# The order of four engines in a memory-attention stage, and who makes two of eight final clips

## The reference, cut to what matters

```python
xi = layernorm(hidden) @ Wq.T                       # 8 heads
for _ in range(3):                                  # NUM_STEPS
    scores = einsum('bhsd,hnd->bhsn', xi, K) * beta # 256 memory slots per head
    w = entmax15(scores)                            # = square(clip(x - tau, 0))
    xi = einsum('bhsn,hnd->bhsd', w, V)
out = xi.transpose(0, 2, 1, 3).reshape(B, S, H * hd) @ Wo.T
# entmax15: tau is the threshold at which sum(square(clip(x - tau, 0))) == 1
```

## Time and profile before

| | us |
|---|---|
| median of three runs | 1848.6 |
| the three runs | 1848.60, 1849.27, 1843.72 |
| profiled execution, its own time | 1844.72 |
| profiled execution, span | 1842.9 |
| first `centre` (unit 0) to last `centre` (unit 47) within the span | 512.02 to 1288.80 |

### The profile page before, as it was taken

The page is one execution under the profiler, slowest core; times in us unless marked ns, Lnnn a source line. Parts: engine busy times, 40 slices in busy tenths (PEclk is TensorE's granted clock), DMA queues, the critical chain, the costliest instruction groups (busy, mean ns, idle before and its releaser), DMA issues. The chain is left out here.

```text
span 1842.9 us, 25960 instructions
## 1 busy us (share of the span) xinstructions
PE 1595.7 (87%) x7554; PEld 1120.9 (61%) x7554; DVE 1375.4 (75%) x3613; ACT 1181.6 (64%) x2865; POOL 601.2 (33%) x1908
## 2 busy tenths in 40 slices
PE   5799999989748889978898879888879899999987
PEld 2546656565646667866786668766645556555554
DVE  6666757562359999999999999999744565776646
ACT  3244343412159999999999999999637665665630
POOL 3504233240134455545554455544310100101000
PEclk9799999999888889999998889988989999999989
DMA  5000000000300000000000000000000000000000
GB/s 227 1 1 1 1 1 1 1 1 0 109 1 1 1 1 1 1 1 1 1 1 1 1 1 1 1 1 1 1 0 1 1 1 1 1 13 1 12 1 23
DMA packets 6717, 19.23 MB, mean 10 GB/s; under 512 B 1072, under 2 KB 4144, under 8 KB 5296
## 3 DMA queue, kind: packets, MB, share of 16 engines
q1 hardware_dynamic: 6576, 17.58, 2.6%
HBM read 15.48 MB, written 2.10 MB: 10 GB/s over the span
## 5 line engine op out<-in xcount | busy, mean ns | idle before, releaser
L1610 ACT ACTIVATE mem_arena<-mem_arena,r_shift 128x256 f32<-128x256 f32 x864 | 385.2, 511 | 23.0 <-POOL r_shift L1529 23.0
L1340 DVE BATCH_NORM_STATS2 r_moments<-mem_arena 128x6 f32<-128x512 f32 x576 | 379.9, 690 | 9.4 <-ACT mem_arena L1610 6.3
L1689 PE MATMUL r_bank<-arena,r_wT 128*128 128x256 f32 x1024 | 232.3, 386 | 4.2 <-ACT mem_arena L1610 3.7
L1689 PEld LDWEIGHTS r_bank<-arena,r_wT 128*128 128x128 f32 x1024 | 195.1, 194 | 35.3 <-issue 9.0
L1705 PE MATMUL r_bank<-ident,mem_arena 128*128 128x128 f32 x576 | 109.6, 322 | 71.8 <-DVE mem_arena L1356 71.7
L1317 DVE MAX8 r_top<-r_bank 128x8 f32<-128x256 f32 x384 | 145.3, 405 | 17.1 <-PE r_bank L1689 16.9
L1699 PE MATMUL r_bank<-arena,ident 128*128 128x256 f32 x384 | 142.4, 458 | 12.6 <-ACT r_wT L1636 12.4
L2243 ACT ACTIVATE arena<-arena,e_NM 128x512 f32<-128x512 f32 (+3 forms) x256 | 134.3, 558 | 29.5 <-DVE e_NM L1931 29.5
L1705 PEld LDWEIGHTS r_bank<-ident,mem_arena 128*128 128x128 f32 x576 | 79.8, 164 | 114.1 <-DVE mem_arena L1356 104.6
L1689 PE MATMUL r_bank<-arena,r_xnT 128*128 128x256 f32 x512 | 120.8, 396 | 24.1 <-ACT mem_arena L1610 23.7
L1610 ACT ACTIVATE r_u<-r_u,r_shift 128x256 f32<-128x256 f32 x288 | 131.8, 510 | 5.6 <-POOL r_shift L1529 5.6
(11 more groups left out here) (328 smaller groups left out, 3222.1 us busy)
## 6 DMA issues: line engine op xcount, KB each, us to landing
w<-in_w SPq DMA_DIRECT2D x3, 1024.0 KB, 14.4
out_x<-X SPq DMA_DIRECT2D x4, 512.0 KB, 2.9
X<-in_x SPq DMA_DIRECT2D x1, 1536.0 KB, 10.6
w_in<-in_w_in SPq DMA_DIRECT2D x1, 1156.0 KB, 6.4
mem_arena<-in_wq SPq DMA_DIRECT2D x1, 1024.0 KB, 17.5
mem_arena<-in_wo SPq DMA_DIRECT2D x1, 1024.0 KB, 21.0
gate<-in_gate SPq DMA_DIRECT2D x1, 1024.0 KB, 7.8
up<-in_up SPq DMA_DIRECT2D x1, 1024.0 KB, 9.8
```

Of the source, the lines that this page charges most:

```text
L1340: last = dve.bn_stats(moments[:, a.lane, 2 * p:2 * p + 2, :].rearrange("p two c -> p (two c)"), u[a.lane][:, 2 * p:2 * p + 2, :].rearrange ...
L1610: last = act.activation(u[a.lane][:, h, :], u[a.lane][:, h, :] if k else scores[:, h, :], ACT.Relu, bias=shift[:, a.lane, h:h + 1])
L1689: last = pe.matmul(scores[:, h, :], lhs, (G1 if a.first else G2)[:, h, i, :], start=i == 0, stop=i == 1)
```

## The change

POOL takes over the final clip of heads 6 and 7 (a new `weights` on POOL, with a semaphore of its own, `pool_weights`); DVE keeps heads 0 to 5. The list `DVE_CLIPS` and DVE's new `clip` are there but empty: no pass 0 to 3 clip moves. All four per-slot orders are written anew. Tile statistics are now made five units ahead of the slot's own unit and output norms five behind (3 and 9 before), so that the slots count from -5 to 53 (59) where they went from -3 to 56 (60). The code that ACT had for making final clips, unused before, is gone. No instruction count changes other than the two clips per unit that change engine.

```diff
--- before.py
+++ after.py
@@ -1192,9 +1192,10 @@
 
 
 WARM = (1, 1, 1, 1)
-DVE_HEADS = (0, 1, 2, 3, 4, 5, 6, 7)
-ACT_HEADS = ()
-FIRST_SLOT, LAST_SLOT = -3, TILES * STEPS - 1 + 9
+DVE_HEADS = (0, 1, 2, 3, 4, 5)
+POOL_HEADS = (6, 7)
+DVE_CLIPS = ((), (), (), ())
+FIRST_SLOT, LAST_SLOT = -5, TILES * STEPS - 1 + 6
 
 NPAIR = NHM // 2
 PASSES = 4
...
@@ -1332,11 +1333,24 @@
                 dve.drain()
                 dve.tensor_reduce(neg8[:, a.lane], back[:, a.lane], AX.X, ALU.max, negate=True).then_inc(bound_ready, 1)
 
+            def clip(a, k, *heads):
+                if not a.live:
+                    return
+                dve.wait_ge(shift_ready[k - 1], of_unit(a))
+                for h in heads:
+                    last = dve.tensor_scalar(u[a.lane][:, h, :], u[a.lane][:, h, :], shift[:, a.lane, h:h + 1], 0.0,
+                                             ALU.add, ALU.max)
+                    if h % 2:
+                        last.then_inc(dve_clipped[k], 1)
+
...
@@ -1391,39 +1405,38 @@
                     first_batch_stats()
                 if n == LAST_SLOT - 1:
                     first_batch_rows()
-                invert(Unit(n - 8), 3)
-                largest(Unit(n - 5), 2)
-                invert(Unit(n - 6), 0)
-                largest(Unit(n - 5), 3)
-                take_moments(Unit(n - 7), 2, 2, 3)
-                largest(Unit(n - 5), 4)
-                weights(Unit(n - 8), 0)
-                invert(Unit(n - 7), 2)
-                largest(Unit(n - 5), 5, 6, 7)
-                weights(Unit(n - 8), 1)
-                take_moments(Unit(n - 6), 1, 0)
-                weights(Unit(n - 8), 2)
-                take_moments(Unit(n - 6), 1, 1, 2)
-                take_moments(Unit(n - 7), 3, 0)
-                weights(Unit(n - 8), 3)
-                take_moments(Unit(n - 6), 1, 3)
-                take_moments(Unit(n - 7), 3, 1)
-                clear(Unit(n - 5))
-                weights(Unit(n - 8), 4, 5)
-                invert(Unit(n - 6), 1)
-                tile_rows(Unit(n - 2))
-                take_moments(Unit(n - 7), 3, 2)
-                bound(Unit(n - 5))
-                weights(Unit(n - 8), 6, 7)
-                take_moments(Unit(n - 7), 3, 3)
-                out_stats(Unit(n - 9))
-                tile_stats(Unit(n + 3))
-                take_moments(Unit(n - 6), 2, 0)
-                take_moments(Unit(n - 5), 0, 0, 1, 2)
-                out_norm(Unit(n - 9))
-                take_moments(Unit(n - 5), 0, 3)
-                take_moments(Unit(n - 6), 2, 1)
-                largest(Unit(n - 4), 0, 1)
+                take_moments(Unit(n - 3), 3, 3)
+                out_stats(Unit(n - 5))
+                tile_stats(Unit(n + 5))
+                invert(Unit(n - 3), 3)
+                take_moments(Unit(n - 1), 0, 0)
+                take_moments(Unit(n - 2), 2, 0)
+                out_norm(Unit(n - 5))
+                take_moments(Unit(n - 1), 0, 1, 2)
+                largest(Unit(n - 0), 0, 1)
+                take_moments(Unit(n - 1), 0, 3)
+                largest(Unit(n - 0), 2)
+                invert(Unit(n - 1), 0)
+                largest(Unit(n - 0), 3)
+                take_moments(Unit(n - 2), 2, 1, 2)
+                largest(Unit(n - 0), 4, 5)
+                take_moments(Unit(n - 2), 2, 3)
+                largest(Unit(n - 0), 6, 7)
+                weights(Unit(n - 3), 0)
+                invert(Unit(n - 2), 2)
+                take_moments(Unit(n - 1), 1, 0, 1)
+                weights(Unit(n - 3), 1, 2)
+                tile_rows(Unit(n + 1))
+                take_moments(Unit(n - 1), 1, 2)
+                take_moments(Unit(n - 2), 3, 0)
+                weights(Unit(n - 3), 3)
+                take_moments(Unit(n - 1), 1, 3)
+                take_moments(Unit(n - 2), 3, 1)
+                clear(Unit(n - 0))
+                weights(Unit(n - 3), 4, 5)
+                invert(Unit(n - 1), 1)
+                take_moments(Unit(n - 2), 3, 2)
+                bound(Unit(n - 0))
 
         @block.gpsimd
         def _(pool):
@@ -1527,6 +1540,14 @@
                 pool.wait_ge(inv_ready[k], of_unit(a))
                 pool.drain()
                 pool.tensor_tensor(shift[:, a.lane], spread[:, a.lane], inv[:, a.lane], ALU.mult).then_inc(shift_ready[k], 1)
+
+            def weights(a, *heads):
+                if not a.live:
+                    return
+                pool.wait_ge(shift_ready[PASSES - 1], of_unit(a))
+                for h in heads:
+                    pool.tensor_scalar(u[a.lane][:, h, :], u[a.lane][:, h, :], shift[:, a.lane, h:h + 1], 0.0, ALU.add,
+                                       ALU.max).then_inc(pool_weights, 1)
 
             def out_rstd(a):
                 if not (a.live and a.last):
@@ -1557,27 +1578,28 @@
             for n in range(FIRST_SLOT, LAST_SLOT + 1):
                 if n == LAST_SLOT - 2:
                     first_batch_norms()
-                running_sum(Unit(n - 5), 2)
-                mean_and_gap(Unit(n - 5))
-                mean_square(Unit(n - 5))
-                add_gap(Unit(n - 5))
-                add_room(Unit(n - 5))
-                second_moment(Unit(n - 6), 1)
-                step_back(Unit(n - 5))
-                newton(Unit(n - 6), 1)
-                start(Unit(n - 5))
-                out_rstd(Unit(n - 9))
-                second_moment(Unit(n - 5), 0)
-                tile_rstd(Unit(n - 1))
-                second_moment(Unit(n - 7), 3)
-                newton(Unit(n - 5), 0)
-                newton(Unit(n - 7), 3)
-                second_moment(Unit(n - 6), 2)
-                newton(Unit(n - 6), 2)
-                centre(Unit(n - 4))
-                square(Unit(n - 4))
-                running_sum(Unit(n - 4), 0)
-                running_sum(Unit(n - 4), 1)
+                add_room(Unit(n - 2))
+                second_moment(Unit(n - 3), 1)
+                step_back(Unit(n - 2))
+                newton(Unit(n - 3), 1)
+                start(Unit(n - 2))
+                second_moment(Unit(n - 4), 3)
+                out_rstd(Unit(n - 6))
+                newton(Unit(n - 4), 3)
+                weights(Unit(n - 4), 6, 7)
+                second_moment(Unit(n - 2), 0)
+                tile_rstd(Unit(n + 2))
+                newton(Unit(n - 2), 0)
+                second_moment(Unit(n - 3), 2)
+                centre(Unit(n - 1))
+                square(Unit(n - 1))
+                running_sum(Unit(n - 1), 0)
+                newton(Unit(n - 3), 2)
+                running_sum(Unit(n - 1), 1)
+                running_sum(Unit(n - 1), 2)
+                mean_and_gap(Unit(n - 1))
+                mean_square(Unit(n - 1))
+                add_gap(Unit(n - 1))
 
         @block.scalar
         def _(act):
...
@@ -1636,30 +1650,30 @@
                     act.activation(wT[:, a.lane, 2 * p:2 * p + 2, :, :], bank[:, TB + p % 2, :], ACT.Square).then_inc(wT_ready, 1)
 
             for n in range(FIRST_SLOT, LAST_SLOT + 1):
-                clip(Unit(n - 3), 2, 0, 1)
-                clip(Unit(n - 2), 0, 0, 1, 2, 3, 4, 5, 6, 7)
-                clip(Unit(n - 3), 2, 2, 3)
-                columns(Unit(n - 5), 2)
-                clip(Unit(n - 3), 2, 4, 5)
-                columns(Unit(n - 5), 3)
-                newton_root(Unit(n - 2), 0)
-                clip(Unit(n - 3), 2, 6, 7)
-                newton_root(Unit(n - 4), 3)
-                clip(Unit(n - 2), 1, 0, 1, 2)
-                tile_columns(Unit(n - 0))
-                newton_root(Unit(n - 3), 2)
-                clip(Unit(n - 2), 1, 3)
-                clip(Unit(n - 3), 3, 0, 1)
-                clip(Unit(n - 2), 1, 4, 5, 6)
-                clip(Unit(n - 3), 3, 2)
-                clip(Unit(n - 2), 1, 7)
-                clip(Unit(n - 3), 3, 3, 4, 5)
-                columns(Unit(n - 4), 0)
-                clip(Unit(n - 3), 3, 6)
-                bound_root(Unit(n - 1))
-                newton_root(Unit(n - 2), 1)
-                columns(Unit(n - 4), 1)
-                clip(Unit(n - 3), 3, 7)
+                clip(Unit(n - 2), 2, 5)
+                newton_root(Unit(n - 1), 0)
+                clip(Unit(n - 2), 2, 6, 7)
+                clip(Unit(n - 1), 1, 0, 1, 2, 3, 4)
+                newton_root(Unit(n - 2), 2)
+                clip(Unit(n - 1), 1, 5, 6, 7)
+                clip(Unit(n - 2), 3, 0, 1, 2, 3, 4, 5)
+                columns(Unit(n - 3), 0)
+                clip(Unit(n - 2), 3, 6, 7)
+                bound_root(Unit(n - 0))
+                newton_root(Unit(n - 1), 1)
+                columns(Unit(n - 3), 1)
+                tile_columns(Unit(n + 1))
+                clip(Unit(n - 1), 2, 0)
+                clip(Unit(n - 0), 0, 0, 1)
+                clip(Unit(n - 1), 2, 1)
+                clip(Unit(n - 0), 0, 2, 3, 4)
+                newton_root(Unit(n - 2), 3)
+                clip(Unit(n - 0), 0, 5)
+                columns(Unit(n - 3), 2)
+                clip(Unit(n - 0), 0, 6, 7)
```

(37 more changed lines are left out.)

8 lines of the change are left out of this document (4 added, 4 removed).

## The result

The changed kernel takes 1876.2 us (median of 4 runs, 1875.4 to 1877.2), the kernel before 1847.0 beside it: ratio 1.0149, 95% interval 1.0128 to 1.0170. It is 29 us slower, and outside the range of 1830 to 1861. The profiled execution has a span of 1875.4 us and an own time of 1877.15.

The account below looks back on a forecast made before the run. Light intervals were taken as bound by DVE, ACT close behind, heavy ones by PE. Light 0, tile -3.4, heavy +0.7, fill and drain +2 gave near -1 us: 1848 against the 1848.6 median, range 1830 to 1861.

Parts of the forecast that it names:

- The cycle of a light interval: New order, from clip 0 through scores, `centre`, pass 3's shift, its clips and `bound_root` back to clip 0: 15.97 us.
- 16.05 for 26 intervals: Light intervals: 15.97 us plus some for PE's slower clock, so no change, 0; bounds -2 and +5 us.
- The ring: Loop of clip 0, scores, `centre`, `add_room`, `bound_root`, clip 0: 14.95 us before, with 1.1 of play; 15.35 after.
- the heavy groups: Four PE-bound intervals after each 12th unit: PE's list stays 17.3 us, extra tile transposes add 0.7 us for three groups.
- the first three intervals: Pipeline fill: the longer chain costs up to 0.4 us in each from the third on; +2 taken for fill and drain together.
- the tile pairs: Two intervals ahead of each heavy four, with new tiles' layer-norm work: -1.1 us a pair, -3.4 for three.
- The drain: End of the stage: keeps its shape, PE with output products, 0 to +2 us; +2 taken for fill and drain together.
- POOL's clip: Final clip moved to POOL: 0.6 us taken; each may last 1.1 before anyone waits, about 0.25 more absorbed later.
- Cost on the path: nothing: POOL's two final clips hidden behind `newton` of pass 3; without that cover 1.2 us an interval.
- rival C: POOL's clips are long: from 1.25 us each they delay pass 0; at 1.6 us, +22 us, 1870; chance 0.05.
- A: Rival: DVE is the real bound, light and tile intervals gain 0.52 us each, 1830, or 1839 by half; chance 0.30.
- B: Rival: slower through DVE's leg up to `bound`, each late 0.1 us costing 3.2; at 0.35, 1859; chance 0.23.

Follow-up runs that it names:

- a_warm: Changed kernel with more dummy products on PE in light units, 5 instead of 1 ahead of pair 0 and 3 instead of 1 ahead of pair 1: 1861.1 us.
- b_nowarm: Kernel before without its single dummy product ahead of each pair of transposes: 1876.2 us, ratio to before 1.0145.
- b_pool1: b_warm with one final clip, head 7, made by POOL behind `start`: 1852.9 us, ratio to before 1.0013.
- b_warm: Kernel before with more dummy products in light units, 3 instead of 1 ahead of pair 0 and 5 instead of 1 ahead of pair 1: 1843.4 us.
- a_stats: Changed kernel with the next stage's first statistics one slot earlier on DVE: 1870.9 us, ratio to before 1.0114.
- a_dve: a_warm with all eight final clips back on DVE and none on POOL: 1862.6 us, ratio to before 1.0064.
- b_lean: Kernel before with 3 and 5 dummies ahead of pairs 0 and 1 in every unit not heavy, none in heavy ones: 1844.1 us, ratio 0.9964.
- a_w0: Changed kernel with 5 dummies instead of 1 ahead of pair 0 alone in light units: 1861.6 us, ratio to before 1.0067.

## Why the prediction was wrong

**Right, at full clock.** The cycle of a light interval, summed from rows of before, was 15.97 us. In a_warm it is 16.07, and each part can be read in ACT's and POOL's timelines there:

```profile
1216.55 2.51 ACT L1633 ACTIVATE mem_arena<-mem_arena,r_shift 128x256 f32<-128x256 f32 x6 [0.42 <-POOL r_shift L1543]
...
1221.41 0.51 ACT L1633 ACTIVATE mem_arena<-mem_arena,r_shift 128x256 f32<-128x256 f32 x1 [0.35 <-POOL r_shift L1543]
1221.83 0.82 ACT L1633 ACTIVATE mem_arena<-r_bank,r_shift 128x256 f32<-128x256 f32 x2
```

```profile
1214.74 0.32 POOL L1469 TENSOR_TENSOR r_fold<-r_top 128x64 f32<-128x64 f32 x1 [0.15 <-DVE r_top L1319]
...
1216.21 0.30 POOL L1543 TENSOR_TENSOR r_shift<-r_spread,r_inv 128x8 f32<-128x8 f32 x1
```

From `centre` to the shift it is 1.77 us (forecast 1.72), from there to clip 0 5.32 (0.04 + 3.68 + 1.56 = 5.28), to the scores, which start at 1222.79, 0.96 (0.97), and to the next `centre` at 1230.82 8.03 (8.00). The waits of 0.42 and 0.35 are those forecast at about 0.5 and 0.4. DVE at 30.46 of 32.23 us is the forecast 94 to 95%.

**The step that failed:** "I take 16.05 for 26 intervals, with some for PE's slower clock in parts of such stretches (mean 0.93)". It made the clock an addend of 0.08, carried over from the old order. The price hangs on where the half clock lies: nothing while it ends ahead of the scores, up to 0.97 us an interval once it reaches into them (0.75 on average over the 24, by a_warm). Shown by a_warm (17.7 us of the intervals' 22.9 come back) and, in the old order, by b_nowarm (17.1 each). The rows for it were there: PE's waits around the transposes were never laid out for the new order, because nobody waits for those transposes. The Trainium skill (TensorE: Matmul & The Clock Gate, "HAM oscillation — how this bites in real kernels") describes products that start slow after each wait of a loop and says that keeping PE busy cures it; the trace agrees in kind, with waits of 2.2 us.

**A second step, of less weight:** "Before, it has 1.1 us of play, and DVE and ACT fill it". Only the path through the top chain had play. The ring closes through ACT too: `newton` of pass 2, ten clips, a `columns`, a clip, `bound_root`, and on to clip 0. That leg is read from the order of calls and the earlier trace rows, no run tests it by itself; b_pool1 shows the play to be nil in the last seven intervals and 0.17 us in the other light ones. At full clock before is therefore 15.75 to 15.95, not 16.05, and the new order's 16.07 is a loss: 781.98 - 772.67 = 9.3 us. By intervals of a_warm and b_warm, the light ones with their 0.12 to 0.32 make 6.4 of it, the heavy groups 3.6 (70.42 against 69.21 before, +1.2 each where +0.2 was forecast), the first three intervals 0.4, and the tile pairs give 1.1 back.

**The drain** was put at 0 to +2 and came to +6.6. "The drain keeps its shape" overlooked that slots were cut from the loop's end, while the next stage's statistics kept their distance from it; a_stats takes 7.4 of that stretch back.

**POOL's clip** was mis-sized, 1.14 us measured against 0.6 taken. In most light intervals it did no harm (a_dve), as its cover of 1.1 plus 0.25 said. But "Cost on the path: nothing" left out `tile_rstd`, which stands behind the clips in four intervals of each group: in two or three of them they cost some 0.25 us each, 1.7 us in all, a small piece of rival C below its bound of 1.25. A did not come (DVE idle, no gain). B has the sign and not the cause: DVE's `bound` is not what ended last.

**The tile pairs** were to give 1.1 us each. At full clock (a_warm, numbers 11 and 12) they take 32.93 against 33.59, 0.7 less; the other two pairs of a_warm, with half clock in their second interval, 33.32 and 33.45. In the changed kernel the half clock makes 34.29 of the first.

Of the 29 us, then, some 15 are the clock (a_warm, by medians) and 5 the drain (a_stats). Of the last 9, 5.2 lie in the 47 intervals (781.98 against 776.78): the 9.3 that the new order costs at full clock, less the 4.1 that before itself lost to its clock. The rest is not placed; medians and single executions are mixed in this sum, and before's profiled one lies 2.3 us under its median. No mix of the new order with its cures (1854 to 1855) came under the old one; b_warm and b_lean, the old order with dummies in its waits, are the best seen, 0.3 to 0.4% under before.

**Open:** why the half clock lasts 3.4 us in most intervals of the old order and 6.8 in those 24 of the new, and why light intervals 4, 5, 17, 18 and 41 of the changed kernel, with waits of 2.2 us and more, had it for 3.4 us only and back ahead of the scores, while numbers 30 and 42, with the same waits of 2.21 and 0.90, never lost it. By a_w0 it is the longer wait that brings the loss about in these intervals, but it does not always.

## What to carry to other kernels

A wait of PE off the path can still cost on it: after laying out a new order, lay out PE's waits as well, and look how far ahead of its next long run the clock is back. Test a suspected clock loss with dummies in the wait, both ways: add them to the slow kernel, take them from the fast one. Give dummies only to waits: in PE-bound intervals they are in the list, and a unit that waits needs them even when it belongs to a PE-bound group. When a loop's slots are renumbered, re-place whatever is pinned to its last slots.

## What the hardware showed unexpectedly

- A wait of 2.2 us, four transposes and a wait of 0.89 were followed by 6.8 us at 0.50 in most light intervals, although PE was busy 4.97 of the 5 us from 873 on. With the first wait filled (a_w0), the second was not followed by it in most. Twice (numbers 30 and 42) neither was.
- PE's slow stretch cost 0.97 us where its scores grew by 0.6: the rest were transposes that nobody had waited for until then.
- A clip of 128x256 with one tensor input takes POOL 1.14 us and DVE 0.34, 3.4 times as long. The Trainium skill (GPSIMD Engine Reference, "4.1 Engine selection") has one-input work there at roughly line rate; this measurement differs, and decides:

```profile
L1549 POOL TENSOR_SCALAR mem_arena<-mem_arena,r_shift 128x256 f32<-128x256 f32 x72 | 81.7, 1146 | 3.5
```
